# A fused graph network, LSTM and graph attention kernel: convolution slots reordered, first LSTM products moved ahead, query halves signalled apart

## The reference, cut to what matters

```
h = relu(adj @ (x @ Wg0 + bg0))          # first adjacency product
h = relu(adj @ (h @ Wg1 + bg1))          # here: adj @ h first (second adjacency product), then Wg1
for p in 1..4:                           # windows of p nodes
    last = lstm(Wih[p-1], Whh[p-1], windows of h)   # gates i, f, g, o; zero start state
    h[:, ends of windows] = last
x = layernorm(x + h)
Q, V = x @ W_lin.T, x @ W_val.T
attention over the edges with leaky_relu(Q[src] + Q[dst]); out = layernorm(x + mixed @ W_out.T)
```

## Time and profile before

| | |
|---|---|
| runs timed | 884.64, 886.42 and 2373.48 us, median 886.42 |
| profiled execution | 886.29 us, its span 884.5 us |
| PE, PEld, DVE, ACT, POOL busy | 97%, 84%, 79%, 68%, 27% of the span |
| mean granted TensorE clock | 0.996 |
| stages (PE) | convolution slots 4.9 to 191.9 us, LSTM phases to 615.8, attention to the end |

### The profile page before, as it was taken

The page is one execution under the profiler, slowest core; times in us unless marked ns, Lnnn a source line. Parts: engine busy times, 40 slices in busy tenths (PEclk is TensorE's granted clock), DMA queues, the critical chain, the costliest instruction groups (busy, mean ns, idle before and its releaser), DMA issues.

```text
span 884.5 us, 15204 instructions
## 1 busy us (share of the span) xinstructions
PE 860.8 (97%) x5228; PEld 744.5 (84%) x5228; DVE 701.1 (79%) x1572; ACT 602.9 (68%) x1117; POOL 235.0 (27%) x562
## 2 busy tenths in 40 slices
PE   8999999989999999999999999999999999999996
PEld 8888888868778789999998887878887898888885
DVE  5888888868888878777777777767887887887986
ACT  3777777767667767767676656666886676776354
POOL 0233333340000000000000001003564455666775
PEclk9999999999999999999999999999999999999999
DMA  4221211000000001000000086776173011111223
GB/s 138 73 60 60 61 60 49 0 1 1 1 1 0 1 1 48 1 1 1 1 2 0 13 178 149 155 164 152 48 167 73 14 37 34 28 37 37 61 61 84
DMA packets 30987, 45.43 MB, mean 51 GB/s; under 512 B 2592, under 2 KB 23744, under 8 KB 27840
## 3 DMA queue, kind: packets, MB, share of 16 engines
q1 hardware_dynamic: 27680, 27.34, 10.5%
q0 software_dynamic: 2304, 16.78, 9.3%
q10 hardware_dynamic: 928, 0.35, 0.2%
HBM read 19.29 MB, written 8.39 MB: 31 GB/s over the span
## 4 chain that ended last, share of the span: by engine, by line
PE 63%; DVE 11%; ACT 4%; issue 3%; POOL 0%; POOLq 0%; DVEq 0%; ACTq 0%
PE psum L503 7%; PE psum L504 7%; PE psum L505 7%; PE psum L1335 7%; PE psum L521 6%; PE psum L517 6%; PE psum L518 5%; PE psum L1259 5%; PE psum L1348 3%; PE psum L1315 2%; ACT work L645 2%; PE psum L1316 2%; PE psum L1276 2%; DVE work L962 1%; DVE work L980 1%
## 5 line engine op out<-in xcount | busy, mean ns | idle before, releaser
L645 ACT ACTIVATE work<-psum,bias 128x512 f32<-128x512 f32 (+1 forms) x408 | 232.3, 623 | 27.2 <-PE psum L521 25.9
L503 PE MATMUL psum<-hT_hi,w_hi 128*128 128x512 f32 (+1 forms) x406 | 148.2, 365 | 3.1 <-ACT work L645 2.6
L504 PE MATMUL psum<-hT_lo,w_hi 128*128 128x512 f32 (+1 forms) x406 | 146.4, 361 | 0.0
L505 PE MATMUL psum<-hT_hi,w_lo 128*128 128x512 f32 (+1 forms) x406 | 146.4, 361 | 0.0
L629 ACT ACTIVATE work<-work 128x512 f32<-128x512 f32 (+1 forms) x112 | 63.8, 570 | 108.0 <-DVE work L969 71.7
L980 DVE TENSOR_TENSOR work<-work 128x512 f32<-128x512 f32 (+1 forms) x111 | 67.9, 612 | 53.9 <-ACT work L629 53.9
L517 PE MATMUL psum<-hs_hi,w_hi 128*128 128x512 f32 (+1 forms) x288 | 103.8, 360 | 1.1 <-DVE hs_hi L914 1.0
L521 PE MATMUL psum<-hs_lo,w_hi 128*128 128x512 f32 (+1 forms) x288 | 104.4, 363 | 0.0
L518 PE MATMUL psum<-hs_hi,w_lo 128*128 128x512 f32 (+1 forms) x288 | 103.2, 358 | 0.0
L1167 POOL DMA_DIRECT2D hT_lo<-hT_hi x8 | 7.5, 934 | 350.5 <-DVE hT_lo L916 329.8
L503 PEld LDWEIGHTS psum<-hT_hi,w_hi 128*128 128x128 f32 x406 | 76.4, 188 | 17.1 <-ACT work L645 4.9
(11 more groups left out here) (225 smaller groups left out, 1921.4 us busy)
## 6 DMA issues: line engine op xcount, KB each, us to landing
work<-x_by_batch SPq DMA_DIRECT2D x32, 256.0 KB, 2.6
x_stage<-x_by_state SPq DMA_DIRECT2D x8, 1024.0 KB, 4.9
hT_lo<-hT_hi POOLq DMA_DIRECT2D x8, 1024.0 KB, 8.5
hT_lo<-x_stage POOLq DMA_DIRECT2D x8, 1024.0 KB, 7.0
out<-x_kept SPq DMA_DIRECT2D x31, 256.0 KB, 2.3
work<-L_gnn_Wih SPq DMA_DIRECT2D x4, 256.0 KB, 2.9
work<-L_gnn_Whh SPq DMA_DIRECT2D x3, 256.0 KB, 3.0
out<-x_kept SPq DMA_DIRECT2D x2, 128.0 KB, 2.3
```

Of the source, the lines that this page charges most:

```text
L503: pe.matmul(out, w_hi[:, w, g, :], xh, start=True, stop=False)
L504: pe.matmul(out, w_hi[:, w, g, :], xl, start=False, stop=False)
L505: mm = pe.matmul(out, w_lo[:, w, g, :], xh, start=False, stop=(t == 0))
L645: op = act.activation(gate[s][g][:, 0:ph.width], psum[:, 4 * s + g, 0:ph.width], ACT.Tanh if g == G else ACT.Sigmoid, bias=bias[:, b:b + 1])
```

## The change

Five edits go together:

1. In a convolution slot PE makes the second adjacency product (`AH`) last, behind the gate products and the product by Wg1. Its high and low parts are therefore made in the next slot: ACT's right behind the relu, DVE's right behind the seed.
2. ACT makes the gates I, G, O in one row and tanh of the cell last; DVE makes the cell product last in every slot. The special order of the drain (`ended`) is gone, so the seed is always ahead of the cell product.
3. ACT and DVE split a weight piece one slot later than PE turns it.
4. `first_input` moves from slot 36 to slot 34, with a semaphore of its own (`first_gates`), which ACT waits on for those two gates.
5. In attention, the queries' low part signals after two of its four operations and again after the fourth; each half of the gather waits for its own half.

```diff
+    FIRST_INPUT = tiles + 2
 # run_tensor, slot(n)
             if has(n - 5):
                 gate_product(G, n - 5)
-            if has(n - 2):
-                k = n - 2
-                pe.wait_ge(S["h1_ready"], k + 1)
-                if k:
-                    pe.wait_ge(S["ahT_ready"], k)
-                for b in range(BT):
-                    mm = pe.matmul(by_batch(psum[:, AH, :])[:, b, :], h1[k % 2][:, b, :], adjT[:, :], start=True, stop=True)
-                mm.then_inc(S["ah_psum"], 1)
-            if n - 5 == tiles - 1:
+            if has(n - 5):
+                gate_product(O, n - 5)
+            if n == FIRST_INPUT:
                 first_input(I, XW, S["xw_ready"])
                 first_input(G, AH, S["ahT_ready"])
-            if has(n - 5):
-                gate_product(O, n - 5)
             if has(n - 3):
...
+            if has(n - 2):
+                k = n - 2
...
+                mm.then_inc(S["ah_psum"], 1)
 # run_scalar, slot(n): behind the relu of tile n-4
+            if has(n - 3):
+                k = n - 3
+                act.wait_ge(S["ah_psum"], k + 1)
+                act.activation(hT_hi[:, block_of(k)], psum[:, AH, :], ACT.Copy).then_inc(S["ahT_hi"], 1)
...
-                gate_of(I, n - 5)
-                gate_of(G, n - 5)
...
+                gate_of(I, k)
+                gate_of(G, k)
+                gate_of(O, k)
+            if n - 1 in piece_slot:
+                cut_piece(piece_slot.index(n - 1))
             if has(n - 5):
                 k = n - 5
-
-                ended = not has(n - 2)
-                if ended:
-                    gate_of(O, k)
                 act.wait_ge(S["c_ready"], k + 1)
                 act.wait_ge(S["h_mul"], CREDIT + k)
                 act.activation(tanh_c[1], cell[1], ACT.Tanh).then_inc(S["tanh_ready"], 1)
-                if not ended:
-                    gate_of(O, k)
 # run_vector, slot(n)
-            ended = not has(n - 2)
-            if ended and has(n - 5):
-                cell_product(n - 5)
-            if has(n - 4) and has(n - 3):
-                seed(n - 3)
+            if has(n - 3):
+                k = n - 3
+                if k:
+                    seed(k)
+                dve.wait_ge(S["ahT_hi"], k + 1)
+                dve.tensor_tensor(hT_lo[:, block_of(k)], psum[:, AH, :], hT_hi[:, block_of(k)].bitcast(F32),
+                                  ALU.subtract).then_inc(S["ahT_ready"], 1)
...
-            if has(n - 5) and not ended:
+            if has(n - 5):
                 cell_product(n - 5)
...
+            if n - 1 in piece_slot:
+                cut_piece(piece_slot.index(n - 1))
 # back
         def gather(k, h):
-            pe.wait_ge(S["xq_ready"], k + 1)
+            pe.wait_ge(S["xq_ready"], 2 * k + h + 1)
...
-            for b in range(BT):
-                op = dve.scalar_tensor_tensor(out=xq_lo[:, b, :], in0=psum[:, Q, b * P:(b + 1) * P], scalar=scale_of(k, b),
-                                              in1=xq_hi[:, b, :].bitcast(F32), op0=ALU.mult, op1=SUB)
-            op.then_inc(S["xq_ready"], 1)
+            for of_half in halves:
+                for b in of_half:
+                    op = dve.scalar_tensor_tensor(out=xq_lo[:, b, :], in0=psum[:, Q, b * P:(b + 1) * P], scalar=scale_of(k, b),
+                                                  in1=xq_hi[:, b, :].bitcast(F32), op0=ALU.mult, op1=SUB)
+                op.then_inc(S["xq_ready"], 1)
```

More of the change, by code:

```diff
@@ L114, in front @@
     BACK_WEIGHTS = 7
+    FIRST_INPUT = tiles + 2
+    assert FIRST_INPUT > piece_slot[-1]
     SORT_COLS, SORT_ROWS, ADJACENT = 8, 12, 16
@@ L194, in front @@
              "xw_psum xw_hi xw_ready h1_psum h1_ready ah_psum ahT_hi ahT_ready h2_psum h2_hi h2_done first_sum seeded "
-             "gates_read f_ready ig_ready tanh_ready fc_done ig_done c_ready h_mul h_hi first_hi h_done tiles_done "
+             "first_gates gates_read f_ready ig_ready tanh_ready fc_done ig_done c_ready h_mul h_hi first_hi h_done tiles_done "
              "rows_loaded cols_loaded a_loaded iota_done a_zero tables_f ecol_done key_done spreads ranks permutes rows_psum rows_ready cols_psum cols_ready "
@@ L399, in first_input @@
             pe.matmul(out, w_hi[:, w, g, :], xl, start=False, stop=False)
-            pe.matmul(out, w_lo[:, w, g, :], xh, start=False, stop=True).then_inc(gate_psum[g], 1)
+            pe.matmul(out, w_lo[:, w, g, :], xh, start=False, stop=True).then_inc(S["first_gates"], 1)
         def slot(n):
@@ L453, in slot @@
                 pe.matmul(out, wg1_lo[:, :], hT_hi[:, cols], start=False, stop=True, skip_group_check=True).then_inc(S["h2_psum"], 1)
+            if has(n - 2):
+                k = n - 2
+                pe.wait_ge(S["h1_ready"], k + 1)
+                if k:
+                    pe.wait_ge(S["ahT_ready"], k)
+                for b in range(BT):
+                    mm = pe.matmul(by_batch(psum[:, AH, :])[:, b, :], h1[k % 2][:, b, :], adjT[:, :], start=True, stop=True)
+                mm.then_inc(S["ah_psum"], 1)
         def first_sum():
@@ L598, in slot @@
             if has(n - 5):
-                if n == 5:
+                k = n - 5
+                if not k:
                     act.wait_ge(S["b_ready"], 1)
-                gate_of(I, n - 5)
-                gate_of(G, n - 5)
[L603 to L606, removed]
+                gate_of(I, k)
[3 more added lines that the diff above has]
+                cut_piece(piece_slot.index(n - 1))
             if has(n - 5):
                 k = n - 5
-                ended = not has(n - 2)
-                if ended:
-                    gate_of(O, k)
                 act.wait_ge(S["c_ready"], k + 1)
@@ L640, in run_scalar @@
                     for g in ((I, G, O) if t == 0 else (F, I, G, O)):
-                        act.wait_ge(gate_psum[g], nf if g == F else n + 1)
+                        if ph is phases[1] and it == 0 and k == 0 and g != O:
+                            act.wait_ge(S["first_gates"], 1 + (g == G))
+                        else:
+                            act.wait_ge(gate_psum[g], nf if g == F else n + 1 if g == O else n)
                         if g == O:
@@ L1256, in project @@
             if k:
-                pe.wait_ge(free, k)
+                pe.wait_ge(*free)
             for b in range(BT):
@@ L1262, in queries @@
         def queries(k):
-            project(k, Q, w_qv[:, 0:P], S["xq_ready"], S["q_psum"])
+            project(k, Q, w_qv[:, 0:P], (S["xq_ready"], 2 * k), S["q_psum"])
         def values(k):
-            project(k, V, w_qv[:, P:2 * P], S["xv_ready"], S["v_psum"])
+            project(k, V, w_qv[:, P:2 * P], (S["xv_ready"], k), S["v_psum"])
         def gather(k, h):
-            pe.wait_ge(S["xq_ready"], k + 1)
+            pe.wait_ge(S["xq_ready"], 2 * k + h + 1)
             if k:
```

4 lines of the change are left out of this document (removed).

## The result

The changed kernel takes 879.86 us in the median of five runs (878.97 to 881.9), the kernel before 886.42; the ratio is estimated at 0.9932, interval 0.992 to 0.9945 (the medians alone give 0.9926), so the change is under 2%, as forecast. The forecast was 880.0. Single runs far above the rest (2373.48 and 1047.69 us of the kernel before, 1044.61 us of e10, which is also its traced run, at a mean granted clock of 0.75) are left out of the ratios and stages. The profiled execution took 879.66 us, its span 877.9, so 6.6 us of span have gone.

The account below looks back on a forecast made before the run. PE was taken as the bound: busy 97%, with no hole in full slots and holes in drain and attention. 886.29 + 0.3 (filling) - 4.85 (drain) - 1.8 (attention) = 879.9, stated as 880.0 us; range 876.5 to 886.0.

Parts of the forecast that it names:

- Full slots, nothing: Convolution slots 6 to 31: no time gained or lost, PE's work staying 5.27 us a slot.
- the ring: Loop through ACT and DVE in full slots (h_mul, cell product, tanh, next h_mul): 5.13 us, 0.14 under PE's slot.
- Filling the pipeline, +0.3: Slots 3 and 4: product by Wg1 waits for a low part made in the same slot, costing 0.3 us.
- The drain, -4.85: Slot 32 to the third LSTM item: 5.1 us less by the worked schedule, 0.25 given back, so 4.85 saved.
- the 0.25 given back: Drain: allowance for the last cell product and first LSTM products meeting POOL's subtraction, 0.25 us.
- the slow clock: Drain: 3.70 us at granted clock 0.56 behind the long PE wait; its loss of 1.6 us was to vanish.
- the first wait: Drain: PE waits 0.85 us before a product by Wg1 for `AH` of tile 30; this hole stays.
- the long hole: Drain: PE's 3.01 us wait before the last product by Wg1, ended by the last tile's seed; claimed gone.
- the schedule: Drain worked step by step for PE, DVE and ACT: third LSTM item 26.5 us after slot 31 starts, 31.63 before.
- What is gained here stays: After the drain: PE is full until 615.8, so the drain's gain is not lost later.
- Attention, -1.8: Attention slots 1 to 12: earlier gathers save 0.44 + 1.05 + some 0.3, summed to 1.8 us.
- there only its idle time can go: Attention slots 3, 4 and 8 to 11: DVE nearly full, so only its idle 0.14 + 0.30 us can be saved.

Follow-up runs that it names:

- e10: Changed kernel with the input product of gate I one slot sooner, in slot 33: 879.8 us, ratio to before 0.9936.
- e6: Changed kernel with ACT's O gate behind the tanh again in slots 5 to 33: 890.89 us, ratio to before 1.0062.
- e3: Kernel before with one pair exchanged: in slot 34 DVE makes the last tile's seed ahead of the cell product: 882.46 us, ratio 0.9961.
- e12: Changed kernel with the cell product ahead of the seed in slots 34 to 36 and `first_input` back in slot 36: 882.47 us, ratio 0.9971.
- e5: Changed kernel with `first_input` back in slot 36: 879.38 us, ratio to before 0.9935.
- e9: Changed kernel with the last convolution tile's h split by DVE instead of POOL: 880.21 us, ratio to before 0.9939.
- e2: Kernel before with only the half signal of the queries' low part added: 884.35 us, ratio to before 0.9978.
- e1: Changed kernel without the half signal; the queries' low part signals once, after its fourth operation: 880.72 us, ratio to before 0.9941.
- e4: Changed kernel with the cell product back ahead of the seed in slots 34 to 36: 881.57 us, ratio to before 0.995.
- e11: Changed kernel with the last tile's h split on DVE and gate I's input product in slot 33: 878.76 us, ratio to before 0.9924.
- e7: Changed kernel with three extra copies of each h on POOL ahead of its subtraction: 904.25 us, ratio to before 1.0219.
- e8: Changed kernel with the queries' low part signalled after each of its four operations: 880.9 us, ratio to before 0.9947.

## Why the prediction was right, point by point

- **Full slots, nothing: right.** 5.28 instead of 5.27; e6 shows that the ring was computed rightly (5.74 worked out, 5.73 measured; for the change itself 5.13, and 5.10 where DVE catches up) and that the new order of the gates pays for the adjacency product's new place.
- **Filling the pipeline, +0.3: right in size.** Slots 2 to 30 are 0.33 longer, 0.20 of it in slots 2 to 5.
- **The drain, -4.85: right, in its mechanism too.** To item 2 it is -5.19, and item 2 starts 26.43 after slot 31, where 26.5 was worked out (-5.1, ahead of the 0.25 given back). The wait of 3.0 us and the slow clock went as said; the first wait is 0.52 instead of 0.85. The prediction put the long hole down to a seed behind a cell product that took 1.67 us, and did not price the two apart. e3 shows 2.5 us for the seed's order, slow clock included; e12 shows 2.4 without it, for the new place of the adjacency product with the new order of the gates. The move of the input products, which the schedule counts among the products that fill slot 34, is worth nothing (e5).
- **"What is gained here stays": wrong by 0.8, of which 0.25 was priced.** 0.51 is lost by the ninth input product, to POOL's last subtraction (e9); that is what the 0.25 was for. Another 0.29 shows in the rest of the LSTM phases, but e2, with the instructions of before up to attention, is 0.17 longer there than before, too. The 0.12 left are no more than that scatter, and what they are stays open.
- **Attention, -1.8: right in the sum (-1.99), wrong inside.** Slots 5 to 7 gained 12.55 - 11.91 = 0.64, not 1.05; slots 3, 4 and 8 to 11 gained 0.24 + 0.72 = 0.96, not 0.44. The step that failed is "there only its idle time can go": DVE, busy 16.61 of 16.91 us, was read as full. Its same 48 operations now take 16.19. PE's own row was the better sign: of its six waits for the low part before, 1.6 us in all, four are in slots 3, 4, 9 and 11, which were held to be full. Before, the gather came 1.9 us after the start of the high part in every slot (the earlier trace rows has one of them); PE's own work would have allowed 2.92 after the queries. So a slot lost whatever the high part came late beyond 2.92 - 1.89 = 1.03, by 0.15 to 0.48. Now the gather can follow the high part by 1.37, and the high part may be 0.5 later at no cost. (In slots 3, 4 and 11 it is later still, 1.69 to 1.83 behind the queries, and there the gather still comes 0.14 to 0.28 late.) In slot 10 of the kernel after it starts 1.49 behind the queries, and the gather still 2.92 behind them (timeline, queries, high part, gather):

```profile
653.27 1.05 PE L1257 MATMUL psum<-w_qv,y_ordered 128*128 128x128 f32 x8
...
654.76 0.69 DVE L1531 TENSOR_TENSOR xq_hi<-psum,rstd 128x512 fp32r<-128x512 f32 x1
...
656.19 0.39 PE L1274 MATMUL psum<-ends,xq_hi 128*128 128x256 f32 x1
```

  DVE needed a later due time, not less work. It was not full before either: in slots 8 to 10 the values' low part (L1550) started 3.09 behind the queries each time, right behind ACT's high part of the values (2.46 + 0.60), and 1.10 to 1.21 behind the queries' low part, where 1.04 to 1.06 is enough in the kernel after. So DVE itself waited there for what PE had made. The Trainium skill's page "Perfetto Trace Analysis", section "Identifying the Most-Contended Engine", calls occupancy, for VectorE, also a fair measure of how close one is to roofline. The 98% here understated what could go: 0.30 us were idle, and 0.72 went.
- **Unpriced: the start-up,** -0.58, which has nothing to do with the change. So the forecast met the time to 0.14 us partly by luck: -0.09 (drain), +0.55 (lost behind it, over the 0.25 priced), -0.19 (attention) and -0.58 (start-up) cancel to -0.3.

## What to carry to other kernels

A wait at the end of a pipeline is first a question of order: write down, for each engine, which instruction the waiting one needs and what stands ahead of it without need, and exchange that pair; here one pair was worth 2.5 us. When a step is put into another place, work out the ring through the engines with its new neighbours, since the changed kernel takes 891 instead of 880 us if the O gate does not go with it. A high busy share of a helper engine in a stretch where another engine sets the pace is not a bound: compare when its result comes with when it is due.

## What was not expected of the hardware

**Two stretches differ from trace to trace with the same instructions.** The start-up takes 10.9 to 11.1 us in e1, e3, e4, e5, e9, e11 and e12, and 12.0 to 12.8 in before, after, e2, e6, e7 and e8. The second product x·Wg0 in before and in e1:

```profile
8.31 2.05 PE L410 MATMUL psum<-wg,work 128*128 128x128 f32 x8 [0.86 <-DMA work<-x_by_batch]
```

```profile
8.44 1.13 PE L412 MATMUL psum<-wg,work 128*128 128x128 f32 x8 [0.86 <-DVE hs_lo L856]
```

The same eight passes run at half the pace in one and at the full one in the other, behind equal waits; the granted clock of the stretch reads 1.00 in both, so there the pace has to be read, not the clock. The other stretch is attention slot 13, behind the wait for the attention row: 5.42 us in eight traces, 6.3 to 6.8 in e4, e5, e8, e11 and e12. In e4 and after:

```profile
668.50:675.28 6.78, 6.77 (x43) 5.61 (x43) 3.91 (x13) 3.21 (x8) 2.94 (x8) 0.75 0.49 99
```

```profile
668.04:673.46 5.42, 5.21 (x43) 4.33 (x43) 3.73 (x13) 3.32 (x8) 3.23 (x8) 1.00 0.65 132
```

The granted clock of the slot is 0.75 in the one and 1.00 in the other. Together the two stretches can move a time by 3 us, which is why edits worth 0.5 us show in stages and not in medians. Each kernel has one trace, so that this goes by execution and not by kernel is not shown; the eleven times of e2, three from 882.63 to 882.94 and eight from 884.15 to 885.97, look like it.
